# Sharing each group's readout between GpSimd and VectorE in the scan of a decoder's second mixer

## The chip, the cores and the metric

The kernel runs on one core of a Trainium2 chip. The metric is the device time of one execution in microseconds (us). Four engines compute: TensorE does matrix products into PSUM, VectorE (DVE in the rows) and GpSimd (POOL) work element by element, ScalarE (ACT) evaluates functions. SyncE (SP) issues the weight transfers. Engines run their own instruction lists and meet only at semaphores.

## The reference

Two decoder layers run on a batch of four sequences of 512 tokens with 512 features. Each layer has a mixer, a second sub-layer and a feed-forward part, each followed by a layer norm. The part that matters here is the mixer of the second layer, a recurrence with 32 heads, each with 8 keys and 16 values:

```
kv = kt[..., :, None] * vt[..., None, :]
ot = jnp.einsum('bhk,bhkv->bhv', rt, S + bonus[None, :, :, None] * kv)
return (S * dt[..., :, None] + kv, ot)
```

For each of the 32 x 8 x 16 = 4096 states of a sequence, the state before token t is multiplied by r of that token (the readout) and summed over the 8 keys of its head. The bonus term is added apart. Then come a normalisation within each head, a gate, an output projection and a layer norm.

## The kernel before

`decoder` (L1575) runs the whole chain once for each of the four sequences: three times in a loop over b (L1727), and once more behind it (L1729). So every stage of the second mixer stands four times in the trace. One sequence works through stages, one after the other; the outputs of a stage are the inputs of the next, and all engines meet at a stage's end. The second mixer's scan is `mix_scan` (L1206). `mix_projections` comes before it, and `mix_output` (L1321), a layer norm (`ln3`), `finish_mixer1` and the next layer's stages come behind it.

`mix_scan` holds time along the free axis, 512 tokens. The 4096 states are cut into G = 8 groups. A group has 128 partitions, 16 heads by 8 keys, and four value columns, so its tiles are 128 x 2048: four stretches of 512 tokens. Group g uses the keys' half q = g // 4 and the values of tile m = g % 4. For each group:

- TensorE spreads four value rows over the 128 partitions into PSUM banks 4 to 7 (`spread`, L1285; matmuls L1294 and L1297). `spread(g + 2)` is issued at the top of round g and waits for VectorE's product of group g + 1, which frees the banks.
- VectorE multiplies the banks by k into `kvb[g % 3]` (L1263). Then it runs one scan instruction over the 2048 elements (L1269), which reads the decays `da[q]` and `kvb` and writes the states to `hh[g % 2]`, shifted by one element. The state before token t therefore stands at place t, and column 0 is zero.
- GpSimd waits for the scan (`scanned`) and multiplies the states by r back into the same `kvb` buffer: `read_states` (L1217, the instruction L1220), called at L1246. It raises `prod`. In the last group alone GpSimd does only two of the four value columns, and VectorE does the other two, right behind its last scan (L1272 and L1273), and raises `last_prod`.
- TensorE waits for `prod` and sums over the keys with four matmuls per group (L1316) into banks 0 to 3. Each shows as two records in the trace. It raises `red`.

The order is written out by hand. A scan of group g waits for `prod` of group g - 2, because it overwrites the states that this readout used. The product L1263 of group g waits for `red` of group g - 3, whose buffer it takes. Behind the loop VectorE waits for the bonus sums (L1310, issued by TensorE just ahead of the last group's sums, semaphore `bon`), makes four products (L1277), and adds the sums (L1281), the last of which needs the last group's `red`. Then `mix_output` begins with the matmuls L1337.

The ring of weights is filled by SyncE (L1225, L122); no transfer touches the tiles of the scan.

Of the kernel before, what the change touches and what calls it, by code (L numbers as in the profile page):

```python
# [216 lines left out]
def high(x):  # L217

    flat = x.bitcast(BF16)
    if len(x.shape) == 3:  # L220
        return flat.rearrange("p k (t two) -> p k t two", two=2)[:, :, :, 1]
    return flat.rearrange("p (t two) -> p t two", two=2)[:, :, 1]


def low(engine, out, x):

    return engine.tensor_tensor(out, x, high(x), ALU.subtract)  # L227
# [20 lines left out]
def stream_block(k, sp, slots_end, last=NSLOTS):  # L248
    k.w.load_until(sp, slots_end, RING - 1, last)
# [956 lines left out]
def mix_scan(nc, k, slots_end, last):  # L1206

    with ExitStack() as ctx:
        rb, rz, decay, vb, kv, scanned, prod, red, zero, vsplit = [
            k.sem(f"mixs_{n}") for n in ("rb", "rz", "decay", "vb", "kv", "scanned", "prod", "red", "zero", "vsplit")]  # L1210
        bon, bv, osum, scaled, last_prod = [k.sem(f"mixs_{n}") for n in ("bon", "bv", "osum", "scaled", "last_prod")]
        blk = ctx.enter_context(nc.Block())
        G = 8
        kvb = [k.bc[:, at:at + 2048] for at in (0, 2048, 6144)]
        NB = len(kvb)

        def read_states(engine, g, a, b):  # L1217

            quartet = lambda region: region.rearrange("p (v t) -> p v t", v=4)[:, a:b, :]
            return engine.tensor_tensor(quartet(kvb[g % NB]), quartet(k.hh[g % 2][:, 0:2048]),  # L1220
                                        k.rr[:, g // 4, None, :].broadcast_to([P, b - a, T]), ALU.mult)

        @blk.sync
        def _(sp):
            stream_block(k, sp, slots_end, last)  # L1225

        @blk.scalar
        def _(act):
            for q in range(2):
                for i in range(4):  # L1230
                    a = act.activation(k.da[q][:, i, 1:T], k.ew[:, q, 1:T], ACT.Exp, scale=-1.0)
                a.then_inc(decay, 1)

            for c in range(KM):
                act.activation(k.offset[:, c, :], k.gg[:, c, :], ACT.Copy, scale=k.gnb[:, c:c + 1])
                act.activation(k.gg[:, c, :], k.gg[:, c, :], ACT.Copy, scale=k.gnw[:, c:c + 1]).then_inc(scaled, 1)

        @blk.gpsimd
        def _(pool):
            pool.memset(k.hh[0][:, 0:1], 0.0)  # L1240
            pool.memset(k.hh[1][:, 0:1], 0.0).then_inc(zero, 1)
            pool.wait_ge(zero, 1)
            pool.wait_ge(rz, 1)
            for g in range(G):
                pool.wait_ge(scanned, g + 1)
                read_states(pool, g, 0, 4 if g < G - 1 else 2).then_inc(prod, 1)  # L1246

        @blk.vector
        def _(dve):
            for m in range(KM):  # L1250
                low(dve, k.vv_lo[:, m, :], k.vv[:, m, :]).then_inc(vsplit, 1)
            for q in range(2):
                dve.scalar_tensor_tensor(out=k.rbk[:, q, :], in0=k.rr[:, q, :], scalar=k.bonus[:, q:q + 1], in1=k.kk[:, q, :],
                                         op0=ALU.mult, op1=ALU.mult).then_inc(rb, 1)
            dve.wait_ge(rb, 2)
            dve.memset(k.rr[:, :, 0:1], 0.0).then_inc(rz, 1)
            dve.wait_ge(zero, 1)
            for g in range(G):
                q = g // 4
                dve.wait_ge(vb, g + 1)  # L1260
                if g >= NB:
                    dve.wait_ge(red, g - NB + 1)
                dve.tensor_tensor(kvb[g % NB].rearrange("p (v t) -> p v t", v=4), k.ps[:, 4:8, :],  # L1263
                                  k.kk[:, q, None, :].broadcast_to([P, 4, T]), ALU.mult).then_inc(kv, 1)
                dve.wait_ge(kv, g + 1)
                dve.wait_ge(decay, q + 1)
                if g >= 2:
                    dve.wait_ge(prod, g - 1)
                dve.tensor_tensor_scan(k.hh[g % 2][:, 1:2049], k.da[q][:, :, :].rearrange("p v t -> p (v t)"), kvb[g % NB], 0.0,  # L1269
                                       ALU.mult, ALU.add).then_inc(scanned, 1)  # L1270

            dve.wait_ge(scanned, G)  # L1272
            read_states(dve, G - 1, 2, 4).then_inc(last_prod, 1)  # L1273

            dve.wait_ge(bon, 1)
            for c in range(KM):
                dve.tensor_tensor(k.oo[:, c, :], k.vv[:, c, :], k.ps[:, 4, :], ALU.mult).then_inc(bv, 1)  # L1277
            for c in range(KM):
                dve.wait_ge(bv, c + 1)
                dve.wait_ge(red, KM + c + 1)  # L1280
                dve.tensor_tensor(k.oo[:, c, :], k.oo[:, c, :], k.ps[:, c, :], ALU.add).then_inc(osum, 1)  # L1281

        @blk.tensor
        def _(pe):
            def spread(g):  # L1285

                q, m = divmod(g, 4)
                pe.wait_ge(vsplit, m + 1)
                if g >= 1:
                    pe.wait_ge(kv, g)  # L1290
                for i in range(4):
                    sel = k.key_rows_b[32 * i:32 * i + 32, q, :]
                    row = slice(32 * i, 32 * i + 32)
                    mm = pe.matmul(k.ps[:, 4 + i, :], sel, high(k.vv[row, m, :]), start=True, stop=False)  # L1294
                    if i == 0:
                        k.w.tell(mm)
                    mm = pe.matmul(k.ps[:, 4 + i, :], sel, k.vv_lo[row, m, :], start=False, stop=True)  # L1297
                mm.then_inc(vb, 1)

            spread(0)  # L1300
            spread(1)
            for g in range(G):
                q, m = divmod(g, 4)
                if g + 2 < G:
                    spread(g + 2)
                if g == G - 1:
                    pe.wait_ge(rb, 2)
                    pe.wait_ge(kv, G)
                    for half in range(2):
                        mm = pe.matmul(k.ps[:, 4, :], k.key_sum[half], k.rbk[:, half, :], start=(half == 0), stop=(half == 1))  # L1310
                    mm.then_inc(bon, 1)
                pe.wait_ge(prod, g + 1)
                for i in range(4):
                    if g == G - 1 and i == 2:
                        pe.wait_ge(last_prod, 1)
                    mm = pe.matmul(k.ps[32 * i:32 * i + 32, m, :], k.key_sum[q][:, 0:32], kvb[g % NB][:, i * T:(i + 1) * T],  # L1316
                                   start=(q == 0), stop=(q == 1), skip_group_check=True)
                mm.then_inc(red, 1)
# [533 lines left out]
```

## Time and profile before

| what | value |
|---|---|
| median of 3 runs | 4762.82 us (4761.82 to 4769.92) |
| the profiled execution's own time | 4765.15 us |
| its span, first to last instruction | 4763.4 us |
| VectorE busy in the span | 3403.7 us (71%) |
| TensorE busy | 3757.2 us (79%) |
| GpSimd busy | 1305.6 us (27%) |
| granted TensorE clock, mean | 0.868 of full |

The profile is one execution. Busy shares are means over stages with different limits, so a change to one stage is to be read from that stage's own rows. Of the profile's queries, the timeline gives for each instruction its start (us from the span's start) and its length, and in square brackets how long its engine had been idle before it and who ended that. Groups by line give busy time and the mean of one. Windows give the busy time of each engine in a stretch and the TensorE clock granted there.

### The profile page before, as it was taken

The page shows a single profiled execution, that of the slowest core. Times are in us where ns is not written, and L with a number is a line of the kernel's source. Part 1 is how long each engine was busy: PE and PEld are TensorE (multiplying, and loading weights), DVE is VectorE, ACT ScalarE, POOL GpSimd, SP SyncE. Part 2 cuts the span into 40 slices and gives each one's busy share as a digit, 9 for nine tenths or more (in the row PEclk, how much of TensorE's full clock was granted, in tenths as well). Part 3 has the DMA queues.
Part 4 walks back from the last instruction along what each step waited for, and adds up shares of the span by engine and source line. Part 5 has one row for each costly group of instructions (what it writes and reads, how often), then busy time and mean ns, then how long its engine had stood idle before and what let it go on. Part 6 is the DMA issues. An engine that isn't in the chain of part 4 may idle for free. (4 is left out here: it accounts for less than half of the span.)

```text
span 4763.4 us, 40552 instructions
## 1 busy us (share of the span) xinstructions
PE 3757.2 (79%) x14900; PEld 1553.9 (33%) x15160; DVE 3403.7 (71%) x2984; ACT 1350.7 (28%) x2044; POOL 1305.6 (27%) x440
## 2 busy tenths in 40 slices
PE   4788779846999769856799768965799967984798
PEld 1222333313333233313333333322333333331443
DVE  4888568575899458676699667766599856967443
ACT  3666232114322232113322123121322133211201
POOL 1444114331344104341144202332144311433000
PEclk8899879867999879968799988976799987986899
DMA  3788202101122202111122211110122120210122
GB/s 144 279 309 318 111 28 79 62 18 42 67 73 73 94 24 73 54 40 49 47 73 73 91 47 53 67 53 22 47 73 73 60 104 27 73 66 20 59 96 73
DMA packets 69896, 385.55 MB, mean 81 GB/s; under 512 B 7744, under 2 KB 7872, under 8 KB 67648
## 3 DMA queue, kind: packets, MB, share of 16 engines
q1 hardware_dynamic: 69696, 382.87, 22.9%
q8 instruction: 127, 2.08, 0.2%
q14 instruction: 73, 0.60, 0.0%
HBM read 318.09 MB, written 64.75 MB: 80 GB/s over the span
## 5 line engine op out<-in xcount | busy, mean ns | idle before, releaser
L825 POOL TENSOR_TENSOR hh<-hh,bc 128x2048 f32<-128x2048 f32 x96 | 449.1, 4678 | 1271.0 <-DVE hh L754 1271.0
L244 PE MATMUL ps<-r,ring 128*128 128x512 bf16 (+1 forms) x1860 | 733.0, 395 | 12.9 <-issue 6.9
L241 PE MATMUL ps<-xr,ring 128*128 128x512 bf16 x1633 | 654.0, 400 | 28.7 <-DVE r L487 15.6
L245 PE MATMUL ps<-xr,ring 128*128 128x512 bf16 x1676 | 670.8, 400 | 2.8
L825 POOL TENSOR_TENSOR bc<-bc 128x2048 f32<-128x2048 f32 x96 | 449.7, 4685 | 605.6 <-DVE bc L754 605.6
L241 PE MATMUL ps<-r,ring 128*128 128x512 bf16 (+3 forms) x1129 | 450.5, 400 | 73.7 <-DVE xc L794 36.6
L712 ACT ACTIVATE da<-ps,params_sb 128x511 f32<-128x511 f32 x768 | 463.0, 691 | 56.3 <-PE ps L608 36.8
L245 PE MATMUL ps<-r,ring 128*128 128x512 bf16 (+4 forms) x1158 | 462.3, 400 | 1.9
L754 DVE TENSOR_TENSOR_SCAN bc<-da,bc 128x2048 f32<-128x2048 f32 x96 | 440.3, 4586 | 0.9
L754 DVE TENSOR_TENSOR_SCAN hh<-da,hh 128x2048 f32<-128x2048 f32 x96 | 438.8, 4571 | 2.4
L749 DVE TENSOR_TENSOR hh<-ps,bc 128x2048 f32<-128x2048 f32 x96 | 218.5, 2276 | 179.3 <-ACT bc L705 131.3
L241 PEld LDWEIGHTS ps<-xr,ring 128*128 128x128 bf16 x1696 | 167.8, 99 | 372.2 <-issue 193.6
L719 ACT ACTIVATE row<-ps 128x512 f32<-128x512 f32 x100 | 59.7, 597 | 802.9 <-PE ps L245 802.9
L244 PE MATMUL ps<-bc,ring 128*128 128x512 bf16 (+2 forms) x463 | 197.5, 426 | 113.0 <-POOL bc L227 64.1
L794 DVE TENSOR_TENSOR xc<-xc,ps 128x512 f32<-128x512 f32 x176 | 120.2, 683 | 232.3 <-PE ps L245 232.3
L244 PEld LDWEIGHTS ps<-r,ring 128*128 128x128 bf16 (+1 forms) x1912 | 189.2, 99 | 237.5 <-issue 30.6
L749 DVE TENSOR_TENSOR bc<-ps,bc 128x2048 f32<-128x2048 f32 x96 | 218.3, 2274 | 54.0 <-PE ps L615 54.0
L608 PE MATMUL ps<-r,squares_sb 32*128 32x512 f32 x384 | 234.1, 691 | 20.6 <-ACT da L712 20.6
L245 PEld LDWEIGHTS ps<-xr,ring 128*128 128x128 bf16 x1696 | 166.7, 98 | 234.4 <-issue 27.6
L615 PE MATMUL ps<-r,squares_sb 32*128 32x512 f32 x384 | 222.7, 661 | 24.3 <-DVE hh L749 14.6
L719 ACT ACTIVATE r<-ps 128x512 f32<-128x512 f32 x96 | 57.3, 597 | 587.8 <-PE ps L245 587.8
L241 PEld LDWEIGHTS ps<-r,ring 128*128 128x128 bf16 (+4 forms) x1160 | 112.7, 97 | 338.3 <-issue 181.3
(218 smaller groups left out, 6147.1 us busy)
## 6 DMA issues: line engine op xcount, KB each, us to landing
ring<-wsplit SPq DMA_DIRECT2D x308, 768.0 KB, 4.2
r<-wstream SPq DMA_DIRECT2D x77, 768.0 KB, 7.2
wsplit<-ring SPq DMA_DIRECT2D x77, 768.0 KB, 5.0
bc<-xT SPq DMA_DIRECT2D x4, 1024.0 KB, 4.8
xr<-xT SPq DMA_DIRECT2D x4, 1024.0 KB, 10.7
bc<-guwT SPq DMA_DIRECT2D x4, 1024.0 KB, 12.6
out<-xr SPq DMA_DIRECT2D x4, 1024.0 KB, 3.9
ctxTs<-ctxT SPq DMA_DIRECT2D x4, 512.0 KB, 3.3
```

The source lines that it names most:

```text
L241: mm = pe.matmul(out, w_hi, x_hi, start=start, stop=False)
L244: pe.matmul(out, w_hi, x_lo, start=False, stop=False)
L245: return pe.matmul(out, w_lo, x_hi, start=False, stop=stop)
L608: pe.matmul(dt_bank, k.headmean[at, :], dt[at, s // 4, :], start=True, stop=True).then_inc(dt_mm, 1)
L615: pe.matmul(dtx_bank, k.headmean[at, :], dtx[at, s // 4, :], start=True, stop=True).then_inc(dtx_mm, 1)
L712: a = act.activation(k.da[s % 2][:, n, 1:T], dt_bank[:, 1:T], ACT.Exp, scale=rate[:, GRP * s + n:GRP * s + n + 1])
L719: act.activation(t2[jt % 2], gate_bank(jt), ACT.Tanh, scale=0.5).then_inc(th, 1)
L749: dve.tensor_tensor(quartet(s), dtx_bank[:, None, :].broadcast_to([P, GRP, T]), k.in_rows, ALU.mult).then_inc(inp, 1)
L754: dve.tensor_tensor_scan(states(s), k.da[s % 2][:, :, :].rearrange("p n t -> p (n t)"), states(s), 0.0, ALU.mult, ALU.add).then_inc(scanne ...
L794: dve.tensor_tensor(k.xc[:, m, :], k.xc[:, m, :], down_bank, ALU.add).then_inc(taken, 1)
L825: pool.tensor_tensor(quartet(s), quartet(s), k.out_rows, ALU.mult).then_inc(read, 1)
```

## The change

In the scan loop of `mix_scan`, GpSimd multiplies value columns 0 and 1 of every group by r, and VectorE multiplies columns 2 and 3 right behind its scan of that group, before it goes on to the next group's product. Until now this split was made in the last group alone. The semaphore `last_prod` becomes `own_prod` and counts all groups. The scan of group g waits for it too, and TensorE waits for it in every group between its second and third sum.

```diff
-        bon, bv, osum, scaled, last_prod = [k.sem(f"mixs_{n}") for n in ("bon", "bv", "osum", "scaled", "last_prod")]
+        bon, bv, osum, scaled, own_prod = [k.sem(f"mixs_{n}") for n in ("bon", "bv", "osum", "scaled", "own_prod")]
...
                 pool.wait_ge(scanned, g + 1)
-                read_states(pool, g, 0, 4 if g < G - 1 else 2).then_inc(prod, 1)
+                read_states(pool, g, 0, 2).then_inc(prod, 1)
...
                 if g >= 2:
                     dve.wait_ge(prod, g - 1)
+                    dve.wait_ge(own_prod, g - 1)
                 dve.tensor_tensor_scan(k.hh[g % 2][:, 1:2049], k.da[q][:, :, :].rearrange("p v t -> p (v t)"), kvb[g % NB], 0.0,
                                        ALU.mult, ALU.add).then_inc(scanned, 1)
-
-            dve.wait_ge(scanned, G)
-            read_states(dve, G - 1, 2, 4).then_inc(last_prod, 1)
+                dve.wait_ge(scanned, g + 1)
+                read_states(dve, g, 2, 4).then_inc(own_prod, 1)
...
                 for i in range(4):
-                    if g == G - 1 and i == 2:
-                        pe.wait_ge(last_prod, 1)
+                    if i == 2:
+                        pe.wait_ge(own_prod, g + 1)
```

## Rows read from the trace of the kernel before

**Rows 1.** Windows: the first sequence's scan loop, first scan's start to last scan's end.
```profile
core 0: us, PE busy (x) PEld busy (x) DVE busy (x) ACT busy (x) POOL busy (x), PEclk, DMA share, GB/s
965.00:1031.60 66.60, 23.23 (x115) 3.82 (x116) 66.32 (x16) 2.55 (x5) 31.54 (x7) 0.50 0.00 0
```

**Rows 2.** Groups by line, whole span: VectorE's scan, GpSimd's readout, VectorE's product.
```profile
L1269 DVE TENSOR_TENSOR_SCAN hh<-da,bc 128x2048 f32<-128x2048 f32 x32 | 204.3, 6385 | 1.1
L1220 POOL TENSOR_TENSOR bc<-hh,r 128x2048 f32<-128x2048 f32 (+1 forms) x32 | 139.6, 4364 | 166.1 <-DVE hh L1269 166.1
L1263 DVE TENSOR_TENSOR bc<-ps,r 128x2048 f32<-128x2048 f32 x32 | 72.5, 2264 | 0.0
```

**Rows 3.** Timeline, first sequence, first two groups: start, length, engine, line.
```profile
962.63 2.29 DVE L1263 TENSOR_TENSOR bc<-ps,r 128x2048 f32<-128x2048 f32 x1
964.96 4.42 DVE L1269 TENSOR_TENSOR_SCAN hh<-da,bc 128x2048 f32<-128x2048 f32 x1
969.30 2.27 DVE L1263 TENSOR_TENSOR bc<-ps,r 128x2048 f32<-128x2048 f32 x1
969.56 4.51 POOL L1220 TENSOR_TENSOR bc<-hh,r 128x2048 f32<-128x2048 f32 x1 [11.06 <-DVE hh L1269]
971.60 6.75 DVE L1269 TENSOR_TENSOR_SCAN hh<-da,bc 128x2048 f32<-128x2048 f32 x1
```

**Rows 4.** Timeline, first sequence, seventh to last group: VectorE and GpSimd.
```profile
1022.61 2.26 DVE L1263 TENSOR_TENSOR bc<-ps,r 128x2048 f32<-128x2048 f32 x1
1022.77 4.51 POOL L1220 TENSOR_TENSOR bc<-hh,r 128x2048 f32<-128x2048 f32 x1 [4.36 <-DVE hh L1269]
1024.90 6.66 DVE L1269 TENSOR_TENSOR_SCAN hh<-da,bc 128x2048 f32<-128x2048 f32 x1
1031.59 1.23 DVE L1220 TENSOR_TENSOR bc<-hh,r 128x1024 f32<-128x1024 f32 x1
1031.64 3.38 POOL L1220 TENSOR_TENSOR bc<-hh,r 128x1024 f32<-128x1024 f32 x1 [4.36 <-DVE hh L1269]
1032.78 2.48 DVE L1277 TENSOR_TENSOR r<-r,ps 128x512 f32<-128x512 f32 x4
1035.17 2.48 DVE L1281 TENSOR_TENSOR r<-r,ps 128x512 f32<-128x512 f32 x4
```

**Rows 5.** The readout's line, whole span: count, then ns min/median/max by engine.
```profile
L1220 POOL TENSOR_TENSOR bc<-hh,r x32: 3382/4502/4510, 969.6 to 4369.7; 128x2048 f32<-128x2048 f32 x28, 128x1024 f32<-128x1024 f32 x4
L1220 DVE TENSOR_TENSOR bc<-hh,r x4: 1224/1226/1226, 1031.6 to 4369.6; 128x1024 f32<-128x1024 f32 x4
```

**Rows 6.** Timeline, TensorE, first sequence: sixth group onwards, up to the next stage.
```profile
1016.15 0.63 PE L1294 MATMUL ps<-r,key_rows_b 32*128 32x512 bf16 x4 [4.62 <-DVE bc L1263]
1016.54 0.67 PE L1297 MATMUL ps<-bc,key_rows_b 32*128 32x512 bf16 x4
1018.46 1.93 PE L1316 MATMUL ps<-bc,squares_sb 128*32 128x512 f32 x8 [1.25 <-POOL bc L1220]
1027.33 1.94 PE L1316 MATMUL ps<-bc,squares_sb 128*32 128x512 f32 x8 [6.94 <-POOL bc L1220]
1029.19 3.54 PE L1310 MATMUL ps<-r,squares_sb 128*128 128x512 f32 x4
1035.08 1.30 PE L1316 MATMUL ps<-bc,squares_sb 128*32 128x512 f32 x8 [2.34 <-POOL bc L1220]
1037.97 5.97 PE L1337 MATMUL ps<-r,squares_sb 128*128 128x512 f32 x8 [1.60 <-PEq L1208]
```

**Rows 7.** Windows behind the scan, first sequence: columns as in rows 1.
```profile
1035.00:1043.00 8.00, 6.33 (x15) 2.38 (x16) 2.65 (x5) 0.00 (x0) 0.02 (x1) 0.57 0.29 98
1043.00:1053.00 10.00, 4.64 (x11) 1.55 (x9) 6.11 (x11) 6.51 (x9) 0.00 (x0) 0.99 0.00 0
1053.00:1059.50 6.50, 3.80 (x9) 1.46 (x11) 5.37 (x7) 0.00 (x0) 4.49 (x4) 0.50 0.00 0
```

## The prediction

> **What bounds the kernel now.** I began with the windows, because the page's busy shares mix all stages. In the scan loop of one sequence VectorE is busy for 66.32 of 66.60 us, GpSimd for 31.54 and TensorE for 23.23 [rows 1]. So VectorE bounds this stage, and the change gives VectorE more to do. Read by busy time alone it must lose. The groups by line say where to look further: the scan takes 6385 ns in the mean [rows 2], over 2048 elements, while the first scan of the sequence takes 4.42 us and the second 6.75 [rows 3]. They have the same shape and the same operands' places, so 2.3 us of the second is not work.
>
> The timeline shows what it is. The second scan starts at 971.60, while GpSimd's readout runs from 969.56 to 974.07 [rows 3]. The scan ends at 978.35, which is 4.28 us behind GpSimd's end. The last scan starts at 1024.90, GpSimd's readout ends at 1027.28, and the scan ends at 1031.56, again 4.28 us behind it [rows 4]. A scan alone takes 4.42. A scan that starts while GpSimd reads the states makes almost no headway until GpSimd is done. It is stopped, not slowed: 2.38 us of overlap lengthen it by 2.24. The product L1263, which has one input in PSUM, stands wholly inside GpSimd's readout and takes 2.26 to 2.27 us, as it takes 2.29 with GpSimd idle [rows 3, 4]; GpSimd's 4.51 shows nothing of it either. So the readout and the scan exclude each other, and the readout and the product don't.
>
> The Trainium skill states this in "SBUF — State Buffer", "Who interferes with whom": a VectorE instruction with two SBUF inputs contends with a GpSimd instruction that reads SBUF, and the one that started first has the port pair for its whole instruction. By that rule the scan waits for GpSimd's end, and the trace agrees: 4.28 us from that end in both groups.
>
> **The period of a group, before.** From scan start to scan start it is (1024.90 - 971.60) / 6 = 8.88 us. By parts: GpSimd starts 0.08 behind a scan's end (1031.56 to 1031.64), reads for 4.51, and the next scan ends 4.28 behind that, together 8.87. Counted from the first scan's start to the last one's end the loop takes 1031.56 - 964.96 = 66.60 us. The first period in it is shorter (971.60 - 964.96 = 6.64), since the first scan runs alone.
>
> **The change, part by part.** The last group before the change already has the new form, once in each of the four sequences, so nearly every price is in the trace.
>
> *VectorE's half readout is added* in seven more groups. It takes 1.226 us, in all four cases between 1224 and 1226 ns [rows 5]. It starts 0.03 us behind the scan's end (1031.56 to 1031.59) and the next instruction starts 1.19 us after it [rows 4]. I take 0.03 + 1.19. The wait on VectorE's own `scanned` also ends the small overlap of neighbouring records: before, the product started 0.08 ahead of the scan's recorded end (969.30 against 969.38), and that is in the 0.03.
>
> *The product* L1263 keeps its place and price. Start to start with the scan behind it takes 2.29 to 2.30 us (971.60 - 969.30, 1024.90 - 1022.61) [rows 3, 4]. One more wait, on `own_prod`, stands ahead of the scan. It is for a group two back, long done. The second group's scan has two waits ahead of it and the seventh's three, and both have the same 2.30 and 2.29: a wait that is already met costs nothing here. Its bounds are 0 and the 0.03 us that a live wait costs.
>
> *GpSimd's readout is halved.* In the last group it takes 3.38 us where half of 4.51 would be 2.26 [rows 4, 5]. The difference is 1.12: now VectorE's half readout starts first, by 0.05 us (1031.59 against 1031.64), and GpSimd stands until it ends at 1032.82; from there it takes 2.20. GpSimd therefore ends 1035.02 - 1031.56 = 3.46 us behind the scan's end.
>
> *The next scan* starts 0.03 + 1.19 + 2.30 = 3.52 us behind the previous scan's end, 0.06 us after GpSimd has finished. The scan then runs alone and takes 4.42 to 4.43. If GpSimd were late, the scan would end 4.28 behind it, as now. That decides from 7.95 - 4.28 = 3.67 us behind the last scan's end, a half readout of 3.59: another 0.2 us of slack.
>
> The new period is 4.43 + 3.52 = 7.95 us. Seven of them and the last scan: 7 x 7.95 + 4.43 = 60.1 us against 66.60. That saves **6.5 us per sequence and 26 us in four**.
>
> *TensorE's waits.* The new wait for `own_prod` stands ahead of the third sum. VectorE's half ends 2.2 us before GpSimd's, so when TensorE has passed `prod`, it is met. Queued behind it are this group's last two sums and the next spread; nothing of VectorE waits for them soon. A spread takes 1.1 us (1016.15 to 1017.21) [rows 6], starting about with the scan, and VectorE wants it 4.43 + 1.22 = 5.65 us after that scan's start: over 4 us of slack. The buffer that `red` frees is wanted two periods later. So this cost is nothing, covered by VectorE; without that cover it would be the wait's 0.03 us.
>
> *The bonus sums* (L1310) are the closest cover. Before, TensorE sums group six from 1027.33 and makes the bonus up to 1032.73, while VectorE wants it at 1032.78 [rows 4, 6]: 0.05 us of slack. After, GpSimd's last but one readout ends 0.06 ahead of the last scan's start, call that t. The sums begin at t, the bonus starts 1.86 later and ends at t + 5.4. VectorE wants it at t + 4.43 + 1.22 = t + 5.65. The slack grows to some 0.25 us. It costs nothing; without its cover it costs a few tenths, four times.
>
> *The tail* (half readouts, last sums, L1277, L1281) is the same instructions at the same distances.
>
> *Moved instructions, transfers, other queues:* no transfer is moved. GpSimd's and SyncE's queues hold nothing else here that anyone waits for.
>
> **Downstream.** The stages behind depend on each other, and each waits for the scan's outputs, so 6.5 us earlier stays 6.5 us earlier, unless TensorE's clock shifts. In the scan loop the granted clock is 0.50, its level of 1.2 GHz [rows 1]. Behind it the clock is 0.57, then 0.99, then 0.50 again [rows 7]. TensorE's work before these changes is the same with the same spacing: sums and bonus for 5.4 us, then 2.35 us of idleness before [rows 6], and 7.95 - 5.4 = 2.5 after. I forecast no shift. The bound: L1337 takes 5.97 us, mostly at the low clock [rows 6]; it could take half that, or a stretch as long that now has the high clock could lose it. That is 3 us either way per sequence, 12 in all.
>
> **Sum.** The profiled execution took 4765.15 us; less 26 gives 4739. The median is 2.3 us below the profiled one, so I predict **4737 us** for the median. A difference of 0.2%, 9.5 us, is about what a measurement of this kernel can tell from no change.
>
> **The rivals.**
>
> *A, GpSimd goes first (slower).* The semaphore that releases both halves is the same, and VectorE leads by 0.05 us only. If GpSimd starts first, VectorE's half waits for all of GpSimd's, some 2.25 us (half of 4.51). Then the period is 4.43 + 0.08 + 2.25 + 1.2 + 2.30 = 10.25, and the loop takes 7 x 10.25 + 4.43 = 76.2, 9.6 more than before: +38 us, 4801. It decides from the point at which VectorE's start falls behind GpSimd's, in the groups before the last. Against it: in all four last groups VectorE's half takes 1224 to 1226 ns and GpSimd's 3.38 [rows 5], with GpSimd idle for 4.36 us before, as it will be in every group. 4%.
>
> *B, busy time counts (slower).* If the later scans' 6.65 us were their own and not GpSimd's doing, each period would be 6.65 + 3.52 = 10.17 and the loop 7 x 10.17 + 6.65 = 77.8, 11.2 more: +45 us, 4808. The Trainium skill advises the opposite of this change in "Perfetto Trace Analysis", "Optimizing Scalar/DVE Operations": with VectorE saturated, work is better offloaded from it, though it adds that between VectorE and GpSimd this might not help. By the first half of that advice the result is B's. Against B: the first scan, with GpSimd idle, takes 4.42, and the stretch follows the overlap. 2%.
>
> *C, GpSimd's half stays long (no change).* If the half took 4.5 us instead of 3.38, held up further by the product or by its own fixed cost, the scan would again end 4.28 behind it and the period would be the old 8.87. Every tenth above 3.59 takes 0.7 us per sequence. In between lies a partial gain. Against it: in the last group four products of the same kind (one input in PSUM) stand behind VectorE's half, and 3.38 holds in all four. No change or nearly: 5%.
>
> *D, the clock shifts.* The gain in the scan comes, but up to 12 us are given back or added: 4725 to 4749. 9% for a shift of over 3 us either way, and still faster.
>
> *The forecast:* 80%.
>
> **How the numbers follow.** Forecast and D lie between 4725 and 4749 and hold 89%. The range leaves out A, B and C, 11% together, and the outer ends of D. I take 4728 to 4748: the runs' own scatter, a GpSimd half of 3.8 us (0.2 above its point, 28 times, 6 us), and most of D. Faster by over 0.2%: 80 + 9 = 89%, of which I give 1 to a large shift: 88. Within 0.2%: C and that shift, 6. Slower: A and B, 6.
>
> **What would show it.** Right: all 32 scans at 4.42 to 4.43 us, in place of four. VectorE's half 32 times at 1.23 and GpSimd's 32 times at 3.38. Scan to scan 7.95 us. The loop 60.1 us, with VectorE still busy throughout. GpSimd's end just before the next scan's start. Wrong: VectorE's half at over 3 us (A), scans still at 6.65 with GpSimd done before they start (B), GpSimd's half at over 3.5 and scans longer than 4.43 (C), VectorE idle ahead of L1277 (the bonus), other lengths of L1337 and of the projection behind it (D).

## The result and the profile after

The changed kernel takes 4736.84 us, the median of 6 runs (4732.29 to 4739.31), against 4765.0 for the kernel before in 6 runs (4761.82 to 4769.92). The ratio is 0.9939, with a 95% interval from 0.9926 to 0.9951. It is faster by 28 us, 0.6%, where 26 and a median of 4737 were forecast. The profiled execution took 4736.57 us, its span is 4734.8 us against 4763.4, and the mean granted clock is 0.871.

The windows of the first sequence, the scan loop first (scan start to the last scan's end), with the columns of [rows 1]:

```profile
core 0: us, PE busy (x) PEld busy (x) DVE busy (x) ACT busy (x) POOL busy (x), PEclk, DMA share, GB/s
967.00:1027.00 60.00, 22.99 (x115) 3.80 (x116) 59.45 (x24) 2.69 (x5) 23.61 (x7) 0.50 0.00 0
1027.00:1035.00 8.00, 4.07 (x12) 0.99 (x11) 6.00 (x9) 0.00 (x0) 3.38 (x1) 0.71 0.08 12
1035.00:1043.00 8.00, 6.56 (x13) 2.58 (x12) 3.69 (x7) 2.95 (x5) 0.00 (x0) 0.82 0.22 87
```

VectorE is as full as before, 59.45 of 60.00 us, but the loop is shorter though seven instructions were added to it: 59.88 us (967.09 to 1022.54 + 4.43) against 66.60. The groups by line of that stretch show why; they answer to [rows 2]:

```profile
L1270 DVE TENSOR_TENSOR_SCAN hh<-da,bc 128x2048 f32<-128x2048 f32 x8 | 35.4, 4426 | 0.3
L1220 POOL TENSOR_TENSOR bc<-hh,r 128x1024 f32<-128x1024 f32 x7 | 23.6, 3373 | 38.3 <-DVE hh L1270 38.3
L1263 DVE TENSOR_TENSOR bc<-ps,r 128x2048 f32<-128x2048 f32 x8 | 18.3, 2284 | 0.0
L1220 DVE TENSOR_TENSOR bc<-hh,r 128x1024 f32<-128x1024 f32 x8 | 9.8, 1225 | 0.3
```

The scan takes 4426 ns in the mean where it took 6385 [rows 2]. The eight half readouts take 9.8 us, seven of them, 8.6 us, inside the loop. The scans give back more than that: eight of them take 35.4 us where they took 51.1 (8 x 6385 ns). The timeline of the last two groups, VectorE's rows and then GpSimd's, stands against [rows 4]:

```profile
1014.62 4.43 DVE L1270 TENSOR_TENSOR_SCAN hh<-da,bc 128x2048 f32<-128x2048 f32 x1
1019.08 1.23 DVE L1220 TENSOR_TENSOR bc<-hh,r 128x1024 f32<-128x1024 f32 x1
1020.22 2.28 DVE L1263 TENSOR_TENSOR bc<-ps,r 128x2048 f32<-128x2048 f32 x1
1022.54 4.43 DVE L1270 TENSOR_TENSOR_SCAN hh<-da,bc 128x2048 f32<-128x2048 f32 x1
1027.00 1.23 DVE L1220 TENSOR_TENSOR bc<-hh,r 128x1024 f32<-128x1024 f32 x1
1028.14 2.47 DVE L1277 TENSOR_TENSOR r<-r,ps 128x512 f32<-128x512 f32 x4
...
1019.12 3.39 POOL L1220 TENSOR_TENSOR bc<-hh,r 128x1024 f32<-128x1024 f32 x1 [4.54 <-DVE hh L1270]
```

From scan to scan it is 1022.54 - 1014.62 = 7.92 us. GpSimd ends at 1022.51 (1019.12 + 3.39), 0.03 us ahead of the scan, so nothing is left to stop the scan. TensorE's timeline answers to [rows 6]:

```profile
1022.56 1.93 PE L1316 MATMUL ps<-bc,squares_sb 128*32 128x512 f32 x8 [4.92 <-POOL bc L1220]
1024.43 3.58 PE L1310 MATMUL ps<-r,squares_sb 128*128 128x512 f32 x4
1030.48 1.39 PE L1316 MATMUL ps<-bc,squares_sb 128*32 128x512 f32 x8 [2.47 <-POOL bc L1220]
1033.32 5.95 PE L1337 MATMUL ps<-r,squares_sb 128*128 128x512 f32 x8 [1.45 <-PEq L1208]
```

**Where the 28.6 us of span went.** Four loops of 59.88 in place of 66.6: 26.9. The tail, from the last scan's end to L1357 (the next stage's first subtraction), fell from 12.4 to 12.3: 0.4 in all. The remaining 1.3 us have nothing to do with the scan. In the rest of the four sequences the two profiles differ in two places only. The first sequence's first scan starts 2.1 us later, at 967.09 against 964.96, and the stretch from the first sequence's L1365 to the second one's first scan is 3.4 us shorter, 1025.92 against 1029.30. The last section comes back to both.

### The profile page after: what moved, and what is told of

It reads as the page before. It is cut to its first block and busy times, and to the rows that moved or that the text cites. A ratio compares the mean times of both kernels' runs of the same rounds, so it can differ in the third digit from the quotient of the medians.

```text
span 4734.8 us, 40864 instructions
## 1 busy us (share of the span) xinstructions
PE 3782.1 (80%) x15160; PEld 1550.9 (33%) x15160; DVE 3377.1 (71%) x3012; ACT 1351.7 (29%) x2044; POOL 1271.9 (27%) x440
## 5 line engine op out<-in xcount | busy, mean ns | idle before, releaser
L244 PE MATMUL ps<-r,ring 128*128 128x512 bf16 (+1 forms) x1912 | 753.2, 394 | 0.0
L241 PE MATMUL ps<-xr,ring 128*128 128x512 bf16 x1696 | 680.6, 401 | 29.7 <-DVE r L227 16.3
L245 PE MATMUL ps<-xr,ring 128*128 128x512 bf16 x1696 | 679.0, 400 | 0.0
L241 PE MATMUL ps<-r,ring 128*128 128x512 bf16 (+4 forms) x1160 | 463.7, 401 | 100.6 <-DVE xc L794 39.2
L245 PE MATMUL ps<-r,ring 128*128 128x512 bf16 (+4 forms) x1160 | 463.1, 400 | 0.0
L241 PE MATMUL ps<-bc,ring 128*128 128x512 bf16 (+3 forms) x416 | 175.4, 422 | 119.1 <-DMA ring<-wsplit 38.2
```

What stands on the lines that cost most here:

```text
L241: mm = pe.matmul(out, w_hi, x_hi, start=start, stop=False)
L244: pe.matmul(out, w_hi, x_lo, start=False, stop=False)
L245: return pe.matmul(out, w_lo, x_hi, start=False, stop=stop)
```

## The experiments

**Does the overlap cost the time?** In the kernel before, each scan also waits for the readout of the group before it:

```diff
-                if g >= 2:
-                    dve.wait_ge(prod, g - 1)
+                if g >= 1:
+                    dve.wait_ge(prod, g)
```

> The kernel before, in which each scan also waits until GpSimd has finished the whole readout of the group before, so that no scan overlaps a readout. Theory (a scan is stopped while GpSimd reads the states): the wait takes the place of the stop. All 32 scans 4.42 to 4.43 us, from GpSimd's end to the scan's end 4.45 to 4.5 instead of 4.28, period 9.06 us, loop 4.42 + 7 x 9.06 = 67.8 us, so about +5 us against before: 4770. Rival (the later scans' 6.65 us are their own or come from TensorE's traffic): the scans stay at 6.65 behind the wait, the loop is 4.42 + 7 x 11.3 = 83.5 us, +68 us: 4833.

Timeline of VectorE and GpSimd in the second and third group (start, length):

```profile
977.39 4.42 DVE L1271 TENSOR_TENSOR_SCAN hh<-da,bc 128x2048 f32<-128x2048 f32 x1 [2.63 <-POOL bc L1220]
981.73 2.27 DVE L1263 TENSOR_TENSOR bc<-ps,r 128x2048 f32<-128x2048 f32 x1
986.53 4.43 DVE L1271 TENSOR_TENSOR_SCAN hh<-da,bc 128x2048 f32<-128x2048 f32 x1 [2.53 <-POOL bc L1220]
...
981.89 4.51 POOL L1220 TENSOR_TENSOR bc<-hh,r 128x2048 f32<-128x2048 f32 x1 [4.63 <-DVE hh L1271]
```

All scans take 4.42 to 4.43 us. What stood as work on VectorE's row now stands as a wait of 2.53 us in brackets, and the scan ends 4.56 us behind GpSimd's end (986.40 to 990.96) instead of 4.28, where 4.45 to 4.5 was expected. The time is 4777.8 us, 14 above before (1.0029, interval 1.0019 to 1.0039), more than the 5 expected. The longer distance makes the loop 68.5 us against 66.6, 7.7 us over four sequences. Another 3.3 lie in the tail, which is 13.26 us against 12.42 in the first sequence: TensorE's last sums took 1.94 us instead of 1.30, and the output matmuls behind them 6.63 instead of 5.97, with a granted clock of 0.54 from 1040 to 1050 us where the kernel before had 0.66 from 1035 to 1045. So here the clock behind the scan did move. The rest is in stages elsewhere. The rival's 4833 is far off. So of the later scans' 6.65 us only 4.42 are their own; the rest was the overlap with the readout.

**Was GpSimd's readout worth anything before?** VectorE reads all four columns, GpSimd none:

```diff
-            for g in range(G):
-                pool.wait_ge(scanned, g + 1)
-                read_states(pool, g, 0, 2).then_inc(prod, 1)
...
-                read_states(dve, g, 2, 4).then_inc(own_prod, 1)
+                read_states(dve, g, 0, 4).then_inc(own_prod, 1)
```

(TensorE waits for `own_prod` ahead of its first sum.)

> The changed kernel with all four value columns read out by VectorE and none by GpSimd. Theory: scans 4.43, readout 2.29, product 2.28, period 9.0 us, loop 67.4 us, and the tail 1.1 us longer, because VectorE's last readout is longer: about +8 us against before, 4772, and 35 us over the changed kernel. GpSimd's whole readout in the kernel before thus bought almost nothing. Rival (the gain of the change came from less work on GpSimd as such): without GpSimd the time is at or below the changed kernel's 4737.

Groups by line, scan loop of the first sequence:

```profile
L1266 DVE TENSOR_TENSOR_SCAN hh<-da,bc 128x2048 f32<-128x2048 f32 x8 | 35.4, 4426 | 0.3
L1220 DVE TENSOR_TENSOR bc<-hh,r 128x2048 f32<-128x2048 f32 x8 | 18.3, 2292 | 0.3
```

It takes 4766.91 us, 1.0004 of before (0.9995 to 1.0014): no difference that could be told. Giving GpSimd the whole readout had freed VectorE of 2.29 us per group and cost it 2.2 us of standing still. The loop was 67.3 us as expected. The tail grew by 0.1 us only, not 1.1, so the expected 4772 was too high. Its output matmuls do start 1.0 us later behind the last scan's end (7.42 us against 6.41), but they take 5.10 us instead of 5.97, with a granted clock of 0.72 over them instead of 0.61. The clock gave that microsecond back, a shift of the kind that rival D describes. Less work on GpSimd alone is not what the change gains by.

**Who pays if GpSimd goes first?** Rival A, made real with one line ahead of VectorE's half:

```diff
+                dve.wait_ge(prod, g + 1)
                 read_states(dve, g, 2, 4).then_inc(own_prod, 1)
```

> The changed kernel in which VectorE's half readout of each group waits until GpSimd's half is done: rival A of the prediction made real. Theory (the two halves exclude each other, and only the order decides who pays): GpSimd's half alone takes 2.2 to 2.3 us instead of 3.38, scans 4.43, period 10.2 us, loop 76 us, tail 2.3 us longer: +48 us against before, 4813. Rival (the halves could overlap if GpSimd started first, and 3.38 is what 1024 elements cost GpSimd): GpSimd's half takes 3.38 alone too, period 11.4 us, loop 84 us, +80 us or more.

Timeline of one group, VectorE and then GpSimd:

```profile
975.09 4.42 DVE L1270 TENSOR_TENSOR_SCAN hh<-da,bc 128x2048 f32<-128x2048 f32 x1
982.04 1.22 DVE L1220 TENSOR_TENSOR bc<-hh,r 128x1024 f32<-128x1024 f32 x1 [2.52 <-POOL bc L1220]
...
979.60 2.34 POOL L1220 TENSOR_TENSOR bc<-hh,r 128x1024 f32<-128x1024 f32 x1 [8.07 <-DVE hh L1270]
```

GpSimd's half alone takes 2.34 us. In the changed kernel it takes 3.38, of which the first 1.19 lie beside VectorE's half (1027.04 to 1028.23) and 2.19 behind it, a little less than the 2.34 alone. The period is 10.41 us (975.09 to 985.50, the next scan), the loop 77.4, and the time 4823.64 us (1.0127 of before, 1.0110 to 1.0144): 60 us slower, 12 more than I expected. The two semaphore steps and the 2.34 against the prediction's 2.25 make the period 0.2 longer than forecast, which is 6 us; the tail is 2.65 us longer instead of 2.3, which is 1.4; and the profile has one step of 3.4 us in a stage elsewhere more than the kernel before, of the kind that the last section shows. Rival A was priced at 4801 in the prediction; made by waits it costs more than that. It is the one real danger of the change, and it does not occur: all 32 of VectorE's halves take 1224 to 1227 ns.

The readout's line in the changed kernel, whole span, with ns min/median/max, answers to [rows 5]:

```profile
L1220 DVE TENSOR_TENSOR bc<-hh,r x32: 1224/1226/1227, 971.6 to 4341.2; 128x1024 f32<-128x1024 f32 x32
L1220 POOL TENSOR_TENSOR bc<-hh,r x32: 3289/3386/3393, 971.7 to 4341.2; 128x1024 f32<-128x1024 f32 x32
```

**Is two and two the right split?** The same kernel again as a reference, then three columns for GpSimd, then one:

> The changed kernel once more, as the reference of this set: 4737 us, 28 us below before, loop 59.9 us.

It took 4737.2 us, before 4763.33: ratio 0.9947 (0.9930 to 0.9964), the loop 59.88.

```diff
-                read_states(pool, g, 0, 2).then_inc(prod, 1)
+                read_states(pool, g, 0, 3).then_inc(prod, 1)
...
-                read_states(dve, g, 2, 4).then_inc(own_prod, 1)
+                read_states(dve, g, 3, 4).then_inc(own_prod, 1)
```

(and TensorE's wait at i == 3; with one column, 0 to 1, 1 to 4 and i == 1)

> The changed kernel with three value columns read out by GpSimd and one by VectorE, in every group. Theory (a scan ends 4.28 us behind a readout that overlaps it): VectorE's part 0.69 us, GpSimd's 4.0 (0.65 of waiting and 3.4 of work), ending 4.1 us behind the scan's end; the next scan starts 2.95 behind it and takes 5.4; period 8.37 us, loop 63.0 us; +12 us against the changed kernel, 4749. Rival (VectorE's added work is a pure cost and the scan was helped by something else): less work on VectorE is faster, period 7.4 us, 15 us below the changed kernel.

> The changed kernel with one value column read out by GpSimd and three by VectorE, in every group. Theory (with no overlap left only VectorE's work counts): VectorE's part 1.76 us, scans 4.43, GpSimd done well before the next scan, period 8.45 us, loop 63.4 us, tail 0.5 us longer; +16 us against the changed kernel, 4753. Rival (scans in the changed kernel still lose something to GpSimd): the scans fall below 4.42 and part of the 16 us comes back.

With three columns, a group of the timeline reads:

```profile
983.45 0.69 DVE L1220 TENSOR_TENSOR bc<-hh,r 128x512 f32<-128x512 f32 x1
984.06 2.28 DVE L1263 TENSOR_TENSOR bc<-ps,r 128x2048 f32<-128x2048 f32 x1
986.38 5.33 DVE L1270 TENSOR_TENSOR_SCAN hh<-da,bc 128x2048 f32<-128x2048 f32 x1
...
983.50 3.93 POOL L1220 TENSOR_TENSOR bc<-hh,r 128x1536 f32<-128x1536 f32 x1 [4.36 <-DVE hh L1270]
```

GpSimd ends at 987.43, the scan at 991.71, 4.28 behind: the constant of the kernel before, with less than half the overlap (1.05 us against 2.38). The loop is 62.5 us and the time 4751.34 (0.9971 of before), 14 above the reference, though VectorE was given less to do. The loops are 10.4 us of that and the tails 2.2: GpSimd's late end now puts the bonus sums late (L1310, 1030.82 to 1034.60), and L1277 waits for them until 1034.64; the output matmuls behind take 6.19 instead of 5.95. With one column, the scans stay at 4426 ns, VectorE's part is 1758 ns, the loop is 63.6 us and the time 4749.94 (0.9973 of before), 13 above the reference where 16 were expected; the tail grew by 0.1 us instead of 0.5. To one side of two and two the scans stand still, to the other VectorE works more; both rivals fall.

**Does GpSimd's late end bound the period?** The next product is put between the scan and VectorE's half:

```diff
                 dve.tensor_tensor_scan(...).then_inc(scanned, 1)
+                if g + 1 < G:
+                    value_product(g + 1)
                 dve.wait_ge(scanned, g + 1)
                 read_states(dve, g, 2, 4).then_inc(own_prod, 1)
```

> The changed kernel with VectorE's next product (one input in PSUM) moved between the scan and VectorE's half readout. GpSimd's half then starts first and runs beside the product. Theory (a product does not exclude GpSimd, VectorE's own work sets the period): GpSimd's half 2.2 to 2.3 us, VectorE's half 1.23 to 1.3, scans 4.43, period 7.9 to 8.0 us, time that of the changed kernel within 3 us, 4737. Rival (GpSimd's late end is what bounds the period, since it ends only 0.03 us ahead of the next scan): with GpSimd done 1.1 us earlier the period falls below 7.9 and the time by over 5 us.

Its timeline from the second scan to the third, and GpSimd's half between them:

```profile
983.92 4.41 DVE L1273 TENSOR_TENSOR_SCAN hh<-da,bc 128x2048 f32<-128x2048 f32 x1
988.26 2.26 DVE L1262 TENSOR_TENSOR bc<-ps,r 128x2048 f32<-128x2048 f32 x1
990.44 1.40 DVE L1220 TENSOR_TENSOR bc<-hh,r 128x1024 f32<-128x1024 f32 x1
991.77 4.41 DVE L1273 TENSOR_TENSOR_SCAN hh<-da,bc 128x2048 f32<-128x2048 f32 x1
...
988.42 2.35 POOL L1220 TENSOR_TENSOR bc<-hh,r 128x1024 f32<-128x1024 f32 x1 [5.50 <-DVE hh L1273]
```

GpSimd's half now runs beside the product and takes 2.35 us. VectorE's half is held for 0.17 by its end (1.40 against 1.23), yet the period falls to 7.85 us (983.92 to 991.77), just below the 7.9 to 8.0 expected. Two steps between instructions became shorter, by 0.1 us each. The instruction behind the scan is now the product, which needs no `scanned` and starts 0.07 us ahead of the scan's recorded end, where the half readout started 0.03 behind it. And the scan now stands behind the half readout and starts 0.07 ahead of its recorded end, where it started 0.04 behind the end of its own product. The loop is 59.4 us and the tail 0.2 longer. The time is 4736.25 us, ratio 0.9940 (0.9923 to 0.9956), the same as the changed kernel within the intervals. Another order gives the same bound, VectorE's own work, and is not shown to beat it.

**One group at a time, or all at once?** Only groups 0 to 3 (and the last) are shared:

```diff
+        shared = lambda g: g < 4 or g == G - 1
...
-                read_states(pool, g, 0, 2).then_inc(prod, 1)
+                read_states(pool, g, 0, 2 if shared(g) else 4).then_inc(prod, 1)
```

(VectorE's half and the waits for `own_prod` only where a group is shared.)

> The changed kernel in which only the groups 0 to 3 (and the last, as before) are shared; in groups 4 to 6 GpSimd reads all four columns. Theory (each shared readout frees the scan behind it and no other): scans 1 to 4 take 4.43 us, scans 5 to 7 take 6.65; loop 4.43 + 4 x 7.92 + 3 x 8.87 = 62.7 us, 3.9 less than before; 15 to 16 us below before, 4748. Rival (the gain is not one of single groups, but of something set once per scan): the loop is near 59.9 or near 66.6 us.

The loop's fifth and sixth scan, whose predecessors are group 3 (shared) and group 4 (not):

```profile
999.94 4.42 DVE L1273 TENSOR_TENSOR_SCAN hh<-da,bc 128x2048 f32<-128x2048 f32 x1
1006.58 6.65 DVE L1273 TENSOR_TENSOR_SCAN hh<-da,bc 128x2048 f32<-128x2048 f32 x1
```

The loop is 62.70 us as worked out, and the time 4747.99 us (0.9964 of before, 0.9950 to 0.9978), 17 below before. Each shared readout frees the one scan behind it, and no other.

**Does any work of GpSimd stop a scan, or only its reading?** Behind each half readout GpSimd sets unused elements to zero, while the next scan runs:

```diff
                 read_states(pool, g, 0, 2).then_inc(prod, 1)
+                if g < G - 1:
+                    for i in range(2):
+                        if g + i:
+                            pool.wait_ge(idle, 2 * g + i)
+                        pool.memset(k.bc[:, 5120:6144], 0.0).then_inc(idle, 1)
```

> The changed kernel in which GpSimd, behind each group's half readout, sets 1024 unused elements per partition to zero, twice, so that it is busy writing while the next scan runs. Nothing is left out. Theory (what stops a scan is GpSimd's reading of SBUF): scans stay at 4.43 us, time 4737 within 3 us. Rival (any GpSimd work in SBUF stops a scan): each of the 28 scans behind it is longer by the length of a memset or two, some 0.9 us each, so +25 to +50 us.

Timeline of the second scan and of what GpSimd does beside it:

```profile
973.90 4.43 DVE L1276 TENSOR_TENSOR_SCAN hh<-da,bc 128x2048 f32<-128x2048 f32 x1
...
973.81 1.96 POOL L1252 MEMSET bc<- 128x1024 f32 x2
```

GpSimd writes from 973.81 to 975.77. It starts 0.09 us ahead of the scan, and the scan takes 4.43 us all the same. All loops are 59.87 to 59.88 us. So GpSimd's writing does not stop the scan, even where it starts first. The Trainium skill has the same distinction in "SBUF — State Buffer", "Who interferes with whom": a VectorE instruction with two SBUF inputs contends with a GpSimd instruction that reads SBUF, not with one that only writes it. The trace agrees: 4.43 us beside the memsets here, 5.33 beside the three-column readout.

But the time is 4749.44 us, 12 above the reference, and neither theory had that. Three more runs were made for it:

> The changed kernel with one more semaphore, named as in the memset experiment, that nothing raises or waits for, and no memset. The memset kernel's scan loops were as long as the changed kernel's, 59.88 us, and its time was still 12 us more, all of it in stretches of 3.4 us where TensorE's clock was low in layer norms far behind the scan. Theory (the memsets are innocent, and the semaphore's clearing at each stage's end shifts the stages against the clock): this kernel too takes 4749. Rival (GpSimd's activity in the scan moves the clock): this kernel takes 4737.

> The memset kernel with one memset of 256 elements per group in place of two of 1024. Theory (the 12 us grow with what GpSimd does in the scan): some 1 to 3 us over the changed kernel, 4738 to 4740. Rival (the mere presence of the instructions in GpSimd's list costs it): 4749. Scans 4.43 us and loop 59.9 us by both.

> The memset kernel unchanged, again, in another set. If its 12 us are its own, 4749 once more, with three or four gaps between scans at 1029 us. If they were a matter of that set, 4737 to 4741.

The semaphore alone gives 4739.13 us, so my theory on its clearing fell. One memset of 256 elements per group gives 4741.46 (4736.59 to 4743.73), and the memset kernel again 4749.16. Each against the kernel before as run beside it, the changed kernel is 26 us below, the one with the semaphore 26, the one with small memsets 22, and the memset kernel 14 both times. The cost comes with the memsets, it repeats, and it is outside the scans. That it grows with their length is likely but not shown: the small memsets' interval (0.9934 to 0.9969) overlaps the changed kernel's. What it looks like stands in the last section; what causes it stays open.

## Why the prediction was right

**The bound.** VectorE bounds the loop, and its 6.65 us scans hold 2.2 us of standing still. This step carried everything. The added wait, the half dose and the split of three columns show it each in its own way: 4.42 us without overlap, 6.65 only behind an unshared group, and an end 4.28 us behind GpSimd wherever they overlap.

**VectorE's half readout**, priced at 0.03 + 1.19: it starts 0.03 behind the scan (1019.05 to 1019.08) and the product starts 1.14 after it. The 1.19 was read in the last group of before, where the next instruction is L1277. But in the changed kernel L1277 too starts 1.14 after (1027.00 to 1028.14). In the kernel before it had waited 0.05 us for the bonus sums, and the prediction priced that wait into every period. This is the 0.05 by which the period was over-estimated. The product's 2.28 instead of 2.26 gives 0.02 back: 7.92 against 7.95.

**The order.** VectorE starts 0.04 us ahead of GpSimd in the rows above (1027.00 against 1027.04), and in all 32 groups its half takes 1224 to 1227 ns, so GpSimd never held it. GpSimd's 3.38 to 3.39 held everywhere but in the first group of a sequence, where GpSimd starts 0.14 behind VectorE (971.69 against 971.55) and takes 3.29. It ends 0.03 ahead of the next scan; 0.06 was forecast.

**The bonus sums** were misread, and the total was not harmed by it. The prediction saw 0.05 us of slack before, from their end at 1032.73 to L1277 at 1032.78. There was none. L1277 starts 0.04 to 0.05 us behind their end in all four sequences of the kernel before, and 0.04 behind it with three columns (1034.60 to 1034.64), where the trace names them as what it waited for. So that distance is the step of the semaphore, and L1277 was waiting. After the change they were to have 0.25 us of slack. They end at 1028.01 and L1277 starts at 1028.14, 0.13 us, of which the step takes 0.05. In the last sequence 0.05 is all there is (4342.26 to 4342.31). The cover held, with next to nothing to spare.

**The sum.** 26 us were forecast. The loops gave 26.9 and the tail 0.4 in the profile; the medians differ by 28. The 0.05 us misread accounts for what the loops gave above the forecast (28 times 0.05 less 28 times 0.02), and L1277's wait that is gone for 0.3 of the tail's 0.4. The median the forecast started from, 4762.82, was 2 us below the one of all six runs, which made 4737 fit to a fraction of a us. That last closeness is luck.

**The rivals.** A did not occur; made by waits, it cost 60 us. The product-between kernel shows that the order can decide the other way too: there GpSimd's half starts first, and VectorE's is the one that is held. B, busy time counts, fell with the scans' 4426 ns. The Trainium skill says in "Perfetto Trace Analysis", "Optimizing Scalar/DVE Operations" that with a saturated VectorE offloading some work may make sense, but between VectorE and GpSimd might not help. Here the reservation holds: the whole readout given to GpSimd gained nothing measurable (1.0004 without it). C had its point at a GpSimd half of 3.59; the three-column split, with 3.93, behaves as C describes. D, the clock behind the scan, did not occur in the changed kernel: L1337 took 5.95 us against 5.97 [rows 6], and the windows at the distances of [rows 7] from the last scan's end have the same clock.

```profile
1030.41:1038.41 8.00, 6.47 (x15) 2.45 (x16) 2.59 (x5) 0.00 (x0) 0.02 (x1) 0.57 0.30 98
1038.41:1048.41 10.00, 4.57 (x11) 1.47 (x9) 6.18 (x11) 6.51 (x9) 0.00 (x0) 0.99 0.00 0
1048.41:1054.91 6.50, 4.25 (x11) 1.50 (x12) 5.30 (x6) 0.00 (x0) 4.57 (x4) 0.50 0.00 0
```

That it would not occur was less sure than "the same work with the same spacing" made it: in the runs where each scan waits and where VectorE reads everything the clock behind the scan did move, and the output matmuls took 0.7 us longer in the one and 0.9 less in the other.

## What to carry to other kernels

An instruction's length in a profile can hold a wait: when the same shape takes 4.4 us once and 6.6 us later, lay the other engines' rows beside it before counting it as work. Where VectorE scans or multiplies two SBUF operands, GpSimd's reads of SBUF beside it were no free help in this kernel; place them beside VectorE's instructions with a PSUM operand, cut them so that they end before the next scan, and see that VectorE's part starts first. When a price is read from one place, check that nothing waits there: a gap of 0.05 us between an engine's end and another's start can be the semaphore's step and not slack. Then price work moved between the two by what it takes from the scans, not by busy shares.

## What the runs showed that I had not expected

Steps of about 3.4 us, in which TensorE's clock is lower, come in some sequences in stages far from the change. In the layer norm behind the quantised products (`ln1`) of the second sequence, the second profile of the changed kernel had the full clock and the memset kernel did not; columns as in [rows 1], one row of each kernel:

```profile
1745.00:1752.00 7.00, 5.79 (x27) 5.00 (x28) 5.21 (x9) 2.52 (x5) 0.00 (x0) 1.00 0.00 0
```

```profile
1747.70:1756.00 8.30, 7.12 (x25) 5.89 (x26) 5.18 (x9) 2.18 (x4) 0.00 (x0) 0.79 0.00 0
```

The first matmuls there (L873) took 3.72 us in the one and 5.41 in the other:

```profile
1746.21 3.72 PE L873 MATMUL ps<-xc,squares_sb 128*128 128x256 f32 x16 [2.61 <-DVE xc L899]
```

```profile
1748.88 5.41 PE L873 MATMUL ps<-xc,squares_sb 128*128 128x256 f32 x16 [1.85 <-DVE xc L899]
```

That is 1.7 us of the step; most of the rest lies in the matmuls just ahead (L1041, 3.51 us against 2.18). The stretch from one sequence's L1365 to the next one's first scan is near 1026 us in some places and 1029.3 in others. The kernel before had one such step in its profile, the changed kernel and its repeat none, the memset kernel 1029.3 twice in its first profile and 1029.3 and 1032.7 in its second. In the stretch before the last sequence's scans both memset profiles had 1029.0 where the changed kernel has 1022.3, two such steps. So the memset kernel's two profiles have four and five steps in three stretches. The steps are not the memsets' alone: the profiles with VectorE reading everything, with one column, with half the groups and with the small memset have one each, the one with GpSimd first has two. GpSimd's memsets, some 13 us of writing per sequence beside the scans, brought more of them on in both sets of runs, although the scans, the tail and some 550 us behind them ran as without. That the time is longer with the memsets was measured twice; by what path they reach the clock was not found.

Ahead of the first scan of the first sequence the profiles differ as well, although no edit touches an instruction that runs ahead of it: the scan starts anywhere from 963.7 us (small memset) to 976.0 (product between), with 964.6 and 967.1 for the changed kernel itself. For a change of under 10 us in this kernel, a time alone would not tell its own effect from such a step; the loops of the profile do.
